# Nodes in runs of 32 per tile, single-tile GpSimd operations, and degree sums as a GpSimd product and a ScalarE sum

## The reference, cut to what matters

```python
H  = (adj != 0);  w = adj[0, :]
Dn = 1 / (H @ w);  Be = 1 / H.sum(axis=0)
conv(x, W, b) = Dn * (H @ (Be * (H.T @ (x @ W.T)))) + b
h  = layer_norm(relu(conv(x, W1, b1)), gamma, beta)
x1 = norm(x + conv(h, W2, b2) + x)                    # norm: mean 0, variance 1
agg = (adj @ x1) / max(adj.sum(-1), 1e-6)
out = norm(x1 + relu(concat(x1, agg) @ WL.T))
```

## Time and profile before

| | us |
|---|---|
| median of 3 runs (lowest, highest) | 1205.99 (1203.76, 1206.09) |
| profiled execution | 1205.56 |
| its span | 1203.8 |
| busy: PE, PEld, DVE | 1122.4, 918.6, 813.1 |
| busy: ACT, POOL | 314.8, 143.9 |

### The profile page before, as it was taken

How to read it: one execution, slowest core, us unless ns; L and a number is a source line. 1 busy time by engine, 2 the same in 40 slices (tenths; PEclk the granted TensorE clock), 3 DMA queues, 4 the chain that set the end, 5 groups by cost and what they waited for, 6 DMA issues and landing times.

```text
span 1203.8 us, 17912 instructions
## 1 busy us (share of the span) xinstructions
PE 1122.4 (93%) x6112; PEld 918.6 (76%) x6112; DVE 813.1 (68%) x1839; ACT 314.8 (26%) x704; POOL 143.9 (12%) x95
## 2 busy tenths in 40 slices
PE   6899997999989998799988999799997999969997
PEld 5769795696867968579785887768786697866976
DVE  6763896648956499555995469954798538985335
ACT  3243201422014220242202431033311333013230
POOL 2102002120021100211010110201102011020100
PEclk9899998999989999899998999999998999989999
DMA  6103411036010361012610215103151032300000
GB/s 258 53 1 141 125 42 62 0 139 139 34 53 0 139 139 52 35 40 100 148 44 35 93 60 135 46 33 139 42 115 70 0 139 72 85 18 1 1 1 36
DMA packets 46213, 86.15 MB, mean 72 GB/s; under 512 B 6000, under 2 KB 35312, under 8 KB 41072
## 3 DMA queue, kind: packets, MB, share of 16 engines
q1 hardware_dynamic: 46192, 85.88, 22.8%
HBM read 77.47 MB, written 8.39 MB: 71 GB/s over the span
## 4 chain that ended last, share of the span: by engine, by line
PE 69%; DVE 27%; issue 2%; ACT 1%; DMA 1%; SPq 0%; DVEq 0%; ACTq 0%
PE bank L676 26%; PE bank L740 11%; DVE adjT L494 9%; PE bank L778 9%; PE bank L800 9%; PE bank L762 9%; DVE HT L499 5%; PE bank L770 2%; DVE o_f L615 2%; DVE xres L619 2%; DVE stats L474 2%; PE bank L786 1%; ACT m_hi L353 1%; DVE unread L449 1%; DVE xres L470 1%
## 5 line engine op out<-in xcount | busy, mean ns | idle before, releaser
L676 PE MATMUL bank<-yv,adjT 128*128 128x257 f32 x1024 | 223.3, 379 | 0.0
L676 PEld LDWEIGHTS bank<-yv,adjT 128*128 128x128 f32 x1024 | 193.6, 189 | 31.7 <-issue 3.8
L358 ACT ACTIVATE small<-mv,small 128x1 f32<-128x1 f32 x192 | 56.6, 295 | 403.5 <-DVE mv L476 307.6
L704 PE MATMUL bank<-x_hi,H 128*128 128x258 f32 x512 | 131.2, 300 | 31.8 <-DVE m_lo L481 23.3
L740 PE MATMUL bank<-HT,m_hi 128*128 128x512 f32 x256 | 120.5, 471 | 35.2 <-DVE m_lo L481 35.2
L481 DVE SCALAR_TENSOR_TENSOR m_lo<-bank,small,m_hi 128x256 fp32r<-128x256 f32 x128 | 61.1, 483 | 127.2 <-ACT m_hi L353 127.2
L704 PEld LDWEIGHTS bank<-x_hi,H 128*128 128x128 f32 x512 | 100.0, 202 | 34.1 <-DVE m_lo L481 24.9
L704 PE MATMUL bank<-x_lo,H 128*128 128x256 f32 x512 | 125.6, 293 | 0.0
L676 PE MATMUL bank<-x_hi,H 128*128 128x256 f32 x512 | 122.6, 283 | 0.0
L676 PE MATMUL bank<-m_hi,HT 128*128 128x256 f32 x512 | 121.7, 280 | 0.0
L676 PE MATMUL bank<-x_lo,H 128*128 128x256 f32 x512 | 121.1, 280 | 0.0
(11 more groups left out here) (77 smaller groups left out, 1648.2 us busy)
## 6 DMA issues: line engine op xcount, KB each, us to landing
raw<-in_adj_dram SPq DMA_DIRECT2D x32, 1024.0 KB, 8.7
adjB<-in_adj_dram SPq DMA_DIRECT2D x224, 128.0 KB, 3.2
x_in<-in_x_dram SPq DMA_DIRECT2D x8, 1024.0 KB, 4.9
out_dram<-xres SPq DMA_DIRECT2D x32, 256.0 KB, 2.5
w_row<-in_adj_dram SPq DMA_DIRECT2D x8, 512.0 KB, 4.0
W2n<-in_L_gnn_W_dram SPq DMA_DIRECT2D x1, 512.0 KB, 3.8
W1n<-in_L_gnn_W_dram SPq DMA_DIRECT2D x1, 512.0 KB, 7.2
WLn<-in_L_gnn_W_dram SPq DMA_DIRECT2D x1, 512.0 KB, 8.1
```

The costliest lines, as they stand in the source:

```text
L358: nc.scalar.activation(std[:, i:i + 1], mv[:, which, i, 1:2], ACT.Sqrt, bias=eps_c)\
L676: last = mm(bank(stage, i)[:, 0:n_cols], lhsT, rhs, start=(k == 0 and part == 0), stop=(k == NT - 1 and part == parts - 1))
L704: last = mm(*args, start=(c == 0 and n == 0), stop=(c == NT - 1 and n == 1))
```

## The change

Node n now lies on partition (n // 256) * 32 + n % 32, in tile (n // 32) % 8. Columns of a tile are four runs of 32. All loads and stores follow, in four DMAs of 32 partitions each where one did before. GpSimd's three operations over eight tiles become eight of one tile each. The degree sums of graphs 1 to 7 become a product on GpSimd (two slots, in m_lo's memory) and a ScalarE copy with an accumulator; VectorE keeps those of graph 0. In graph 0 ScalarE copies raw into tile order for TensorE's transposes. build_rDn of graphs 1 to 7 stands behind VectorE's loop.

```diff
-   raw <- adj[b] "(p t) e -> p t e", one DMA for two tiles
+   for a in range(NB):
+       sp.dma_start(raw[a * Q:(a + 1) * Q, 2 * j:2 * j + 2, :],
+                    adj[b, a * RB + 2 * j * Q:a * RB + (2 * j + 2) * Q, :]
+                    .rearrange("(t r) e -> r t e", r=Q)).then_inc(raw_loaded[j], 16)
    (x_in and out in the same way, 4 DMAs each where 1 was)
 def load_adjB(b, t):
-    rows = adj[b, :, :].rearrange("(k r t) e -> t r k e", k=NB, t=NT)
+    rows = adj[b, :, :].rearrange("(k t r) e -> t r k e", k=NB, t=NT)
 ...
     sp.wait_ge(H_ready, (b + 1) * NT + t + 1)
-    sp.wait_ge(dn_ready, (b + 1) * NT + t + 1)
     load_adjB(b + 1, t)
@@ gpsimd
+    for t in range(NT):      # split_x; residual likewise, 8 + 8 instructions
+        nc.gpsimd.tensor_tensor(x_lo[:, t, :], x_in[:, t, :], x_hi[:, t, 0:D].bitcast(F32), ALU.subtract)
 ...
     if more:
         split_x(b + 1)
+        pool.wait_ge(w_loaded, (b + 1) * 16 + 16)
+        pool.wait_ge(*full("S4", NT - 1, b))
+        for c in range(NT):
+            pool.wait_ge(H_ready, (b + 1) * NT + c + 1)
+            if c >= 2:
+                pool.wait_ge(dn_ready, (b + 1) * NT + c - 1)
+            nc.gpsimd.tensor_tensor(
+                masked[:, c % 2, :].rearrange("p (k t r) -> p k t r", k=NB, t=NT),
+                H[:, c, :].bitcast(F32).rearrange("p (t k r) -> p k t r", t=NT, k=NB),
+                w_row[:, :].rearrange("p (k t r) -> p k t r", k=NB, t=NT), ALU.mult).then_inc(w_masked, 1)
@@ scalar
+    def order_raw(c):
+        act.wait_ge(raw_loaded[c // 2], 16 * NB)
+        if c >= 2:
+            act.wait_ge(bank_full[TRANSPOSE_BANKS[1]], W_FILLS + c - 1)
+        nc.scalar.activation(ordered[:, c % 2, :].rearrange("p (t k r) -> p t k r", t=NT, k=NB),
+                             raw[:, c, :].rearrange("p (k t r) -> p t k r", k=NB, t=NT), ACT.Copy)
+    (order_raw(0), (1), then take_adjT(c), order_raw(c + 2) in turn)
 ...
+    def sum_Dn(c):
+        act.wait_ge(w_masked, b * NT + c + 1)
+        nc.scalar.activation(masked[:, c % 2, :], masked[:, c % 2, :], ACT.Copy,
+                             accum_out=dn[:, c:c + 1]).then_inc(dn_ready, 1)
     for i in range(NT):
         (yv i, x1T i + 2)
+        if more and i >= 4:
+            sum_Dn(i - 4)
     for i in range(NT):
+        if more and i < 4:
+            sum_Dn(i + 4)
         root("o", 2, std_o, i, b)
@@ vector
-    H[:, c, :] "p (t n) -> p t n" <- raw[:, c, :] "p (n t) -> p t n"
+    H[:, c, :] "p (t k r) -> p t k r" <- raw[:, c, :] "p (k t r) -> p t k r"
-    adjT <- transpose(adjB[:, t, :, :].rearrange("p k (c j) -> p j k c", c=Q))
+    adjT <- transpose(adjB[:, t, :, :].rearrange("p k (j c) -> p j k c", c=Q))
+    dve.wait_ge(bank_full[TRANSPOSE_BANKS[1]], W_FILLS + NT)    # graph 0, ahead of the first m_lo
     if more:
-        dve.wait_ge(q_split, b * NT + NT)
         for c in range(NT):
             build_H_tile(c, b + 1)
-            sum_Dn(c, b + 1)
-        build_rDn(b + 1)
     (the loop of one round per L tile)
     if more:
+        build_rDn(b + 1)
         (HT rows, rBe, m_lo)
@@ tensor
-    graph 0: transposes of raw[:, c, :] with a step of 8; one wait for all of x_lo
+    graph 0: transposes of ordered[:, c % 2, 128 columns]; a wait for each tile of x_lo
```

More of the change, by code:

```diff
@@ L118, in graph_net @@
         m_hi, _, _ = place("m_hi", [P, NT, D], F32R)
-        m_lo, _, _ = place("m_lo", [P, NT, D], F32R)
+        m_lo, m_lo_at, _ = place("m_lo", [P, NT, D], F32R)
         x_in, _, _ = place("x_in", [P, NT, D], F32)
@@ L140, in graph_net @@
         adjB, _, _ = place("adjB", [P, NT, NB, RB], F32, raw_at)
+        ordered, _, _ = place("ordered", [P, 2, C], F32, m_lo_at)
+        masked, _, _ = place("masked", [P, 2, C], F32, m_lo_at)
         yv, _, _ = place("yv", [P, NT, YP], F32, HT_at)
@@ L171, in graph_net @@
         adjB_loaded = [sem(f"adjB_loaded{n}") for n in range(NT)]
-        adjT_ready = sem("adjT_ready")
+        adjT_ready, raw_ordered, w_masked = (sem(n) for n in ("adjT_ready", "raw_ordered", "w_masked"))
         x_loaded, w_loaded, W2_loaded, W1_loaded, WL_loaded, rows_loaded, bias_loaded, table_loaded = (
@@ L246, in load_x @@
             def load_x(b):
-                sp.dma_start(x_in[:, :, :], x[b, :, :].rearrange("(p t) d -> p t d", t=NT)).then_inc(x_loaded, 16)
+                for a in range(NB):
+                    sp.dma_start(x_in[a * Q:(a + 1) * Q, :, :],
+                                 x[b, a * RB:(a + 1) * RB, :].rearrange("(t r) d -> r t d", r=Q)).then_inc(x_loaded, 16)
             def load_w(b):
@@ L268, in graph @@
                     load_w(b + 1)
-                    sp.wait_ge(xb_ready, b + 1)
-                    sp.wait_ge(x_split, b + 1)
+                    sp.wait_ge(xb_ready, b * NT + NT)
+                    sp.wait_ge(x_split, b * NT + NT)
                     load_x(b + 1)
@@ L279, in graph @@
                     sp.wait_ge(normed["o"], b * NT + 2 * j + 2)
-                    sp.dma_start(out[b, :, :].rearrange("(p t) d -> p t d", t=NT)[:, 2 * j:2 * j + 2, :],
-                                 xres[:, 2 * j:2 * j + 2, :]).then_inc(out_stored, 16)
+                    for a in range(NB):
+                        sp.dma_start(out[b, a * RB + 2 * j * Q:a * RB + (2 * j + 2) * Q, :]
+                                     .rearrange("(t r) d -> r t d", r=Q),
+                                     xres[a * Q:(a + 1) * Q, 2 * j:2 * j + 2, :]).then_inc(out_stored, 16)
             over_graphs(sp, graph)
-            sp.wait_ge(out_stored, 16 * (NT // 2) * B)
+            sp.wait_ge(out_stored, 16 * NB * (NT // 2) * B)
         @block.gpsimd
@@ L298, in split_x @@
                 pool.wait_ge(x_hi_done, b + 1)
-                nc.gpsimd.tensor_tensor(x_lo[:, :, :], x_in[:, :, :], x_hi[:, :, 0:D].bitcast(F32), ALU.subtract)\
-                  .then_inc(x_split, 1)
-            pool.wait_ge(x_loaded, 16)
+                for t in range(NT):
+                    nc.gpsimd.tensor_tensor(x_lo[:, t, :], x_in[:, t, :], x_hi[:, t, 0:D].bitcast(F32), ALU.subtract)\
+                      .then_inc(x_split, 1)
+            pool.wait_ge(x_loaded, 16 * NB)
             pool.wait_ge(bias_loaded, 16 * 2)
             def residual(b):
[L307 to L311, removed]
+                for t in range(NT):
+                    nc.gpsimd.tensor_tensor(xres[:, t, :], x_in[:, t, :], x_in[:, t, :], ALU.add).then_inc(xb_part, 1)
+                for t in range(NT):
+                    pool.wait_ge(xb_part, b * NT + t + 1)
+                    nc.gpsimd.tensor_tensor(xres[:, t, :], xres[:, t, :], b2_row[:, :], ALU.add).then_inc(xb_ready, 1)
             residual(0)
@@ L334, in split_x_hi @@
             def split_x_hi(b):
-                act.wait_ge(x_loaded, b * 16 + 16)
+                act.wait_ge(x_loaded, b * (16 * NB) + 16 * NB)
                 nc.scalar.activation(x_hi[:, :, 0:D], x_in[:, :, :], ACT.Copy).then_inc(x_hi_done, 1)
@@ L368, in take_adjT @@
                       .then_inc(bank_empty[tb], 1)
-            for c in range(NT - 1):
+            def order_raw(c):
[3 more added lines that the diff above has]
+                nc.scalar.activation(ordered[:, c % 2, :].rearrange("p (t k r) -> p t k r", t=NT, k=NB),
+                                     raw[:, c, :].rearrange("p (k t r) -> p t k r", k=NB, t=NT), ACT.Copy)\
+                  .then_inc(raw_ordered, 1)
+            order_raw(0)
+            order_raw(1)
+            for c in range(NT - 2):
                 take_adjT(c)
+                order_raw(c + 2)
+            take_adjT(NT - 2)
             take_m_hi("S1", 0, 0, 0)
@@ L437, in build_H_tile @@
             def build_H_tile(c, b):
-                dve.wait_ge(raw_loaded[c // 2], b * 16 + 16)
-                nc.vector.tensor_scalar(H[:, c, :].rearrange("p (t n) -> p t n", t=NT),
-                                        raw[:, c, :].rearrange("p (n t) -> p t n", t=NT), 0.0, None,
+                dve.wait_ge(raw_loaded[c // 2], b * (16 * NB) + 16 * NB)
+                nc.vector.tensor_scalar(H[:, c, :].rearrange("p (t k r) -> p t k r", t=NT, k=NB),
+                                        raw[:, c, :].rearrange("p (k t r) -> p t k r", k=NB, t=NT), 0.0, None,
                                         ALU.not_equal).then_inc(H_ready, 1)
             def sum_Dn(c, b):
+                dve.wait_ge(raw_loaded[c // 2], b * (16 * NB) + 16 * NB)
                 if c == 0:
@@ L494, in transpose_blocks @@
                 nc.vector.transpose(adjT[:, :, t * P:(t + 1) * P],
-                                    adjB[:, t, :, :].rearrange("p k (c j) -> p j k c", c=Q)).then_inc(adjT_ready, 1)
+                                    adjB[:, t, :, :].rearrange("p k (j c) -> p j k c", c=Q)).then_inc(adjT_ready, 1)
             def build_HT_rows(k, b):
@@ L524, in _ @@
             dve.wait_ge(x_hi_done, 1)
-            nc.vector.tensor_tensor(x_lo[:, :, :], x_in[:, :, :], x_hi[:, :, 0:D].bitcast(F32), ALU.subtract)\
```

(16 more changed lines are left out.)

5 lines of the change are left out of this document (1 added, 4 removed).

## The result

| | before | changed |
|---|---|---|
| median (lowest to highest), us | 1204.88 (1203.58 to 1206.09) | 1140.43 (1138.25 to 1140.87) |
| profiled execution's span | 1203.8 | 1138.2 |
| mean granted TensorE clock | 0.967 | 0.997 |
| busy: PE, DVE, ACT, POOL | 1122.4, 813.1, 314.8, 143.9 | 1101.2, 683.9, 382.7, 321.6 |

The ratio is 0.946 (95% interval 0.944 to 0.948): 64.5 us faster, against 58 forecast.

A forecast was written before the change was run, and what follows sets the result against it. TensorE was taken to stand at each of seven graph transitions for VectorE's late m_lo, behind slow transposes and blocked HT rows. 1205.6 - 55 (transitions) - 4 (prologue) + 1.3 (tail) = 1147.9, said as 1148 us; range 1117 to 1196.

The forecast's parts named there:

- The total: Whole kernel: 1205.6 less 55 and 4 plus 1.3 gives 1147.9, said as 1148 us; chance 0.64.
- the seven transitions: Between graphs, TensorE ends S2's first chunk at 490.5 instead of 498.4: 7.9 us saved, seven times, 55.
- The transpose: VectorE's L494 in stage L, reading runs of 32: 1.27 us instead of 2.067, 6.4 us less per graph.
- Slip by the products: VectorE's L loop: GpSimd's late products hold up L619 and L470 of tile 0, 2.5 us per graph.
- HT rows and residual: GpSimd in single tiles: two long blocks (5.5 us per graph) go; five HT rows pay about 0.35 each, 1.7.
- TensorE's waits: S2 after each transition: about 1 us each for m_lo 5 and 6, under 3 us per graph.
- Prologue: Graph 0: last raw pair near 32 us, VectorE at 39 instead of 44.5; 4 us gained, bounds 0 and 8.
- Tail: End of kernel: the last store becomes four issues of up to 0.5 us instead of one, +1.3 us.
- The sums: Degree sums leave VectorE before its L loop; with faster H tests 5.5 us, off the path, covering products 0 and 1.
- A: Rival: the transpose stays at 2.07 us; 1.5 us per graph, 1192 us in all; chance 0.14.
- B: Rival: long GpSimd products delay ScalarE's roots, deciding from 5.0 us each; at 5.5, 1231 us; chance 0.08.
- C: Rival: no collisions, HT rows slip through, TensorE runs without a gap; 11.8 us per transition, 1117 us; chance 0.14.

The follow-up runs named there:

- run 1: Kernel before with only the block transpose's reading order changed to runs of 32 elements (later data wrong, only time read): 1154.72 us, ratio 0.958.
- run 6: Changed kernel with transposes of tile pairs reading in steps of 1, 2, 4 and 8 elements; only transpose durations read, no total time given.
- run 7: Changed kernel with ScalarE's degree sums begun one V tile sooner (sum i - 3 behind yv i): 1123.95 us, ratio 0.934.
- run 3: Changed kernel with degree sums back on VectorE ahead of its loop and GpSimd's operations over eight tiles again, so layout alone: 1164.14 us, ratio 0.966.
- run 4: Changed kernel with only the degree sums and their inverse back on VectorE ahead of its loop (layout and tiles): 1119.28 us, ratio 0.929.
- run 9: Changed kernel with sums back on VectorE and graph 0's residual later, raw now loaded by one 128-partition DMA per tile: 1144.27 us, ratio 0.949.

## Why the prediction was right, and where not

- *The total.* 64.5 us against 58 is nearer than its terms: the seven transitions gave 65 us and not 55, graph 0 gave 1 and not 4, the tail cost 0.5 and not 1.3. That the first two errors have opposite signs is luck.
- *The transpose.* Right in mechanism (runs 1 and 6) and size: 1.22 us, 1.27 forecast. It was costed from H and HT, two instructions of another kind, which the step lengthened 1.60 times (1.093 / 0.685); it lengthened the transpose 1.70 times (2.067 / 1.216). That the share carried over was a guess that held. The 1.27 itself stands beside a computed 1.30 without a reason.
- *Slip by the products.* 2.5 us forecast; 0.55 + 1.64 = 2.2 measured. It fell on L661 of tiles 0 and 1, not on L470 of tile 0 (L513 now, 0.40 us), and run 7 removed nearly all of it. A product takes 2.45 us when alone (2.3 forecast).
- *HT rows and residual.* 1.7 us forecast, 0.27 + 0.28 + 0.39 = 0.9 measured: three rows were held, not five. build_rDn costs 0.6 (0.7). The last m_lo comes 45.4 us behind the loop's start, not 46.9: that is the 1.4 us per graph by which 9.3 exceeds 7.9. TensorE's waits come to the 2 us forecast, but they stand in another place: 1.17 us for m_lo 3, which frees bank 3 (see run 1), 0.66 for m_lo 6 and 0.18 for m_lo 7, not 1 each for 5 and 6. The sum didn't suffer, since m_lo 7 ends the chunk either way; runs 1 and 3, where m_lo 3 is late, missed by it. As forecast, no stretch at the lower clock is left: from 459 to 470 the granted clock is 1.00.
- *Prologue.* 1.0 instead of 4 in the profiled execution (its bounds were 0 and 8). The last pair of raw came at 35.9 us, not 32: the rate of the earlier trace rows was right (210 GB/s in window 371 to 391, 241 in the prologue), but I set x, weights and rows that share the engines too low. VectorE's m_lo 0 was out 2.5 us sooner (44.25, not 46.77), of which TensorE gave back 1.5: it ran the last 32 S1 matmuls behind its wait at a granted clock of 0.70, in 5.6 us instead of 4.1. The stretch of before (the clock is the third number from the end):

```profile
47.31:51.40 4.09, 4.08 (x33) 4.09 (x34) 3.46 (x14) 2.56 (x6) 0.00 (x0) 1.00 0.79 280
```

The same stretch of the changed kernel:

```profile
44.79:50.39 5.60, 5.60 (x33) 5.60 (x34) 4.42 (x16) 2.96 (x7) 5.60 (x9) 0.70 0.01 3
```

It is not the same in every execution. Run 4, whose code up to here is the change's, ran the same 32 matmuls in 4.09 us and started S2 at 48.15 (start, length, what), run 7 at 47.80: gains of 3.3 and 3.6 us, near the 4 forecast.

```profile
44.06 4.09 PE bank L735 x32
48.15 10.27 PE bank L773 x44
```

- *Tail.* 0.5 instead of 1.3. I had let three more issues and their 1.3 us stand in full; why they cost less is not shown.
- *The sums.* "It pays nothing by itself" was right and too kind: I weighed the move only by its slip within the change, and didn't ask what the kernel would be without it. Run 4 answers: TensorE's 2 us of waits per graph are all owed to the slip and the later inverse, and without them the kernel is bound by TensorE, 2.8 us per graph sooner (134.6, not 137.4).
- *Rivals.* A falls with the transpose's 1.22; B with products of 2.45 us, far from 5; C, a TensorE without gaps, is not what the change does, but it is what run 4 does.

## What to carry to other kernels

Price an instruction by its reading step as well as by its size: here a step that left each 4-byte read alone in 16 bytes made the transpose take 1.7 times as long, and one rearrangement of the data removed it everywhere. Cut GpSimd work that overlaps VectorE into pieces as short as the wait you can bear, since each HT row of 0.68 us that met a long one waited it out, up to 3.8 us. Before moving work off a busy engine, check that it is on the path: here the move put its helper in the way of the engine it was to relieve, and cost 21 us. And when a stage seems free to start, look at the banks that it writes as well as at its inputs: S2 waited for a bank that I had left out.

## What the runs showed of the hardware

- VectorE's transpose of 128 x 1024 fp32: 1.21 us at steps of 4 and 8 bytes, 1.99 at 16 (run 6); at 32 bytes 1.99 to 2.03 for the first five tiles of a transition and 2.13 to 2.21 for the last three (the kernel before).
- An instruction with two SBUF inputs (L661, 0.43 us) waited out a GpSimd product and took 2.07 us, and an HT row, with one input, waited out a longer GpSimd instruction and took 3.77 (run 1). The one transpose seen beside a product kept 1.25 (run 7: 418.53 to 419.78, the last two products filling 415.24 to 420.11).
- GpSimd's product over runs of 32 elements costs 2.45 us for 1024 elements, 2.4 ns each, within the 1.8 to 2.6 ns of its 2048-element instructions; ScalarE's copy with an accumulator 1.05 us and 0.19 for its reading.
- A DMA whose source splits as 4 x 32 moved 105 GB/s over 128 partitions; four DMAs of 32 partitions each moved 210 (run 9).
